# Softmax maxima negated on GpSimd between pieces of its other attention work; inverse of the denominators on VectorE

## What is computed

```python
scores = jnp.einsum('bthd,bshd->bhts', q, k)
mask = jnp.tril(jnp.ones((T, T), dtype=scores.dtype))
scores = scores * mask
attn = jax.nn.softmax(scores / T ** 0.5, axis=-1)
out = jnp.einsum('bhts,bshd->bthd', attn, v).reshape(B, T, H * Dh)
return out @ Wo
...
x = _layernorm(x + _L0_attn_ref(x, ...), axis=-1)
```

## Time and profile before

| | us |
|---|---|
| median of 3 runs | 1091.71 |
| lowest and highest | 1091.14, 1093.73 |
| span of the profiled execution (its own time isn't given apart from it) | 1090.9 |
| TensorE busy | 1037.0 |
| VectorE busy | 738.5 |
| ScalarE busy | 486.3 |
| GpSimd busy | 294.7 |

### The profile page before, as it was taken

How to read it: one execution, slowest core, us unless ns; L and a number is a source line. 1 busy time by engine, 2 the same in 40 slices (tenths; PEclk the granted TensorE clock), 3 DMA queues, 4 the chain that set the end, 5 groups by cost and what they waited for, 6 DMA issues and landing times.

```text
span 1090.9 us, 18063 instructions
## 1 busy us (share of the span) xinstructions
PE 1037.0 (95%) x6022; PEld 839.6 (77%) x6023; DVE 738.5 (68%) x1769; ACT 486.3 (45%) x905; POOL 294.7 (27%) x496
## 2 busy tenths in 40 slices
PE   7889998999999885999999999999999999999996
PEld 6667776777777664888888888888888888888885
DVE  5898699778868986566747546545565536654666
ACT  5688488758857884222324222131222122221124
POOL 2186348545733641223210006000000000000224
PEclk9999999999999998999999999999999999999998
DMA  8877267727743732224541003210020000100102
GB/s 260 237 200 204 78 199 200 197 83 188 199 117 117 207 143 77 79 77 164 175 162 61 1 1 40 39 39 1 1 77 12 27 0 33 45 1 1 39 27 89
DMA packets 55216, 106.18 MB, mean 97 GB/s; under 512 B 6240, under 2 KB 8288, under 8 KB 55136
## 3 DMA queue, kind: packets, MB, share of 16 engines
q1 hardware_dynamic: 50256, 90.99, 29.7%
q0 software_dynamic: 4880, 14.18, 3.4%
HBM read 72.11 MB, written 30.94 MB: 94 GB/s over the span
## 4 chain that ended last, share of the span: by engine, by line
PE 57%; DVE 2%; ACT 1%; issue 0%; DMA 0%; POOL 0%; POOLq 0%; DVEq 0%
PE f_bank L53 55%; PE f_bank L1714 1%; PE f_bank L1722 1%; PE f_bank L1793 1%; PE f_bank L1738 0%; DVE ln_stats L1104 0%; DVE rows_kept L2150 0%; ACT rows_kept L1132 0%; DVE h L2116 0%; DMA rows<-sorted_dram 0%; DVE rows_kept L2139 0%; DVE h L2056 0%; DVE rows_kept L1111 0%; POOL out L1660 0%; ACT fsg L1936 0%
## 5 line engine op out<-in xcount | busy, mean ns | idle before, releaser
L1896 ACT ACTIVATE fsg<-f_bank 128x512 f32<-128x512 f32 x64 | 38.2, 598 | 295.6 <-PE f_bank L53 289.2
L2056 DVE TENSOR_TENSOR h<-f_bank,fsg 128x512 f32<-128x512 f32 x64 | 44.2, 691 | 181.6 <-PE f_bank L53 181.4
L714 ACT ACTIVATE probs<-bank,nmax 128x384 f32<-128x384 f32 (+3 forms) x256 | 131.7, 549 | 21.4 <-DVE nmax L899 19.3
L883 DVE CUSTOM_DVE_ANT_0 bank<-bank,mask 128x384 f32<-128x384 f32 (+3 forms) x256 | 122.9, 502 | 13.8 <-PE bank L510 13.0
L521 PE MATMUL bank<-ident,probs 128*128 128x128 f32 x640 | 108.7, 284 | 24.6 <-DVE pt_lo L908 10.7
L1137 POOL TENSOR_SCALAR ln_var<-ln_mv 128x1 f32<-128x1 f32 x39 | 8.9, 229 | 438.8 <-DVE ln_mv L1106 437.4
L908 DVE TENSOR_TENSOR pt_lo<-bank,pt_hi 128x512 f16<-128x512 f32 (+1 forms) x192 | 114.7, 598 | 16.7 <-ACT pt_hi L724 16.4
L724 ACT ACTIVATE pt_hi<-bank 128x512 f16<-128x512 f32 (+1 forms) x192 | 104.9, 546 | 23.5 <-PE bank L521 22.9
L53 PE MATMUL bank<-x_hi,w_qk 128*128 128x512 f32 x256 | 101.5, 414 | 6.7 <-DVE x_lo L913 6.3
L53 PE MATMUL f_bank<-wd_hi,hs_lo 128*128 128x512 f32 x256 | 100.0, 391 | 0.0
L53 PE MATMUL f_bank<-wd_lo,hs_hi 128*128 128x512 f32 x256 | 99.9, 390 | 0.0
(11 more groups left out here) (275 smaller groups left out, 2445.7 us busy)
## 6 DMA issues: line engine op xcount, KB each, us to landing
big_lo<-q_hi_dram SPq DMA_DIRECT2D x32, 256.0 KB
big_lo<-q_lo_dram SPq DMA_DIRECT2D x32, 256.0 KB
big_lo<-k_hi_dram SPq DMA_DIRECT2D x32, 256.0 KB, 3.8
big_lo<-k_lo_dram SPq DMA_DIRECT2D x32, 256.0 KB, 5.1
rows<-sorted_dram SPq DMA_DIRECT2D x19, 256.0 KB, 2.6
q_hi_dram<-q_hi SPq DMA_DIRECT2D x16, 256.0 KB, 3.0
q_lo_dram<-q_lo SPq DMA_DIRECT2D x16, 256.0 KB, 2.9
k_hi_dram<-k_hi SPq DMA_DIRECT2D x16, 256.0 KB, 3.5
```

The source lines that it names most:

```text
L714: ins = act.activation(probs[u % RP][:, at:at + cols(r)], S[u % SR][:, at:at + cols(r)], ACT.Exp, bias=nmax[:, r, c:c + 1])
L883: dve.tensor_tensor_reduce(out=S[u % SR][:, at:at + cols(r)], in0=S[u % SR][:, at:at + cols(r)], in1=mask[:, T - cols(r):T], scale=1.0, sc ...
L1896: act.activation(fsg[v % 2][:, :], GB[v % 2][:, :], ACT.Silu).then_inc(s_sg, 1)
L2056: dve.tensor_tensor(h[r % 2][:, j, :], UB[v % 2][:, :], fsg[v % 2][:, :], ALU.mult).then_inc(s_h, 1)
```

## The change

The negated maxima of units 4 to 47 of each batch move from VectorE to GpSimd; units 0 to 3 stay on VectorE. `negated` now takes the engine. A case for units 24, 27 and 30, in which VectorE negated two columns in two instructions, falls away. GpSimd's attention work is written anew as a loop over units: the negation of u+2 first, and behind it whatever stands at that unit. The sums of head c come at unit 3c+6, the low parts of the next x at units 23, 25, 26 and 28, and `norm_heads` for group m is cut into four steps at units 16, 17, 19 and 20, each plus 12m. Its inverse is now a reciprocal on VectorE at units 17, 29 and 41 (`heads_inverse`), and the constant of -1 is gone. The statistics of row block 3 and the scatters of row blocks 2 and 3 move from behind a batch into units 3 and 6 of the next one. TensorE, ScalarE and SyncE have the same instructions in the same order.

```diff
+        x_lo_at = {23: 0, 25: 1, 26: 2, 28: 3}
+        SUMS_BEHIND = 2 * UPH
+        NORM_FROM = SUMS_BEHIND + (HPT - 1) * UPH + 1
...
+            def norm_step(b, m, step):
...
+                if step == 0:
+                    pool.wait_ge(s_c, b * NM + m + 1)
+                    pool.tensor_tensor(den[:, :, hs], c_up[:, :, hs], n_up[:, :, hs], ALU.mult).then_inc(s_t[0], 1)
...
+                elif step == 1:
...
+                    pool.tensor_tensor(o_tmp[0][:, :, :, :], tail, above, ALU.mult).then_inc(s_t[0], 1)
+                elif step == 3:
...
+                    pool.tensor_tensor(o_here, o_here, o_tmp[0][:, :, :, :], ALU.add).then_inc(s_t[0], 1)
+                elif step == 4:
...
+                    pool.tensor_tensor(o_raw[:, :, hs, :], o_raw[:, :, hs, :],
+                                       rinv[:, :, hs].unsqueeze(3).broadcast_to([P, NB, HPT, HD]),
+                                       ALU.mult).then_inc(s_on[0], 1)
...
             for b in range(B):
                 more = b < B - 1
...
+                for u in range(UPB):
+                    if AHEAD_S < u + AHEAD_MAX < UPB:
+                        negated(pool, b, u + AHEAD_MAX)
+                    if b > 0 and u == LAST_ROW_AT + 1:
+                        ln.rstd(pool, b * NB - 1, NB - 1)
+                    if b > 0 and u - 1 in rows_at:
+                        place(b - 1, rows_at[u - 1])
+                    if u in x_lo_at and more:
+                        x_lo(b + 1, x_lo_at[u])
+                    if u % UPH == 0 and u >= SUMS_BEHIND:
+                        head_sums(b, (u - SUMS_BEHIND) // UPH)
+                    if NORM_FROM <= u < NORM_FROM + (NM - 1) * UPM:
+                        norm_step(b, (u - NORM_FROM) // UPM, (u - NORM_FROM) % UPM)
...
+            def heads_inverse(b, m):
+
+                hs = slice(m * HPT, (m + 1) * HPT)
+                dve.wait_ge(s_t[0], (b * (NM - 1) + m) * 5 + 2)
+                dve.reciprocal(rinv[:, :, hs], den2[:, :, hs]).then_inc(s_t[0], 1)
...
-                    if fresh:
-                        negated(b, u + AHEAD_MAX)
+                    if fresh and u + AHEAD_MAX <= AHEAD_S:
+                        negated(dve, b, u + AHEAD_MAX)
+                    if u >= NORM_FROM and (u - NORM_FROM) % UPM == 1 and u < NORM_FROM + (NM - 1) * UPM:
+                        heads_inverse(b, (u - NORM_FROM) // UPM)
```

More of the change, by code:

```diff
@@ L265, in sum_parts, with negated, last_heads_normed @@
             eng.tensor_tensor(o_raw[:, :, c, :], part[0], part[1], ALU.add).then_inc(s_os[side], 1)
-        def norm_heads(eng, side, b, m):
-            per_batch = (NM - 1, 1)[side]
-            n = (b * per_batch + (m if side == 0 else 0)) * 5
+        def negated(eng, b, u):
+            m, h, rows = units[u]
+            c = m * HPT + h
+            rs = slice(rows[-1], rows[0] + 1, 2) if len(rows) > 1 else slice(rows[0], rows[0] + 1)
+            eng.wait_ge(s_mx, (b * HEADS + c) * NB + rows_done[u % UPH])
+            if rows[0] < NB - 1:
+                eng.tensor_scalar(nmax[:, rs, c:c + 1], smax[:, rs, c:c + 1], 0.0, -1.0, ALU.max,
+                                  ALU.mult).then_inc(s_nm, 1)
+            else:
+                eng.tensor_scalar(nmax[:, rs, c:c + 1], smax[:, rs, c:c + 1], -1.0, None,
+                                  ALU.mult).then_inc(s_nm, 1)
+        def last_heads_normed(eng, b):
+            m = NM - 1
+            side = 1
+            n = b * 5
             hs = slice(m * HPT, (m + 1) * HPT)
@@ L285, in norm_heads @@
             link(eng.tensor_tensor(den[:, :, hs], c_up[:, :, hs], n_up[:, :, hs], ALU.mult))
[L286 to L290, removed]
-            link(eng.tensor_tensor(den2[:, :, hs], den[:, :, hs], rsum[:, :, hs], ALU.add))
[L292 to L297, removed]
+            link(eng.tensor_tensor(o_tmp[side][:, :, :, :], tail, above, ALU.mult))
+            sum_parts(eng, side, b, HEADS - 1)
+            eng.wait_ge(s_os[1], PRIMED + 3 * (b + 1))
+            eng.wait_ge(s_os[0], PRIMED + 3 * (b + 1) * ALONE)
+            link(eng.tensor_tensor(den2[:, :, hs], den[:, :, hs], rsum[:, :, hs], ALU.add))
+            link(eng.reciprocal(rinv[:, :, hs], den2[:, :, hs]))
             link(eng.tensor_tensor(o_raw[:, 0:NB - 1, hs, :], o_raw[:, 0:NB - 1, hs, :], o_tmp[side][:, :, :, :],
@@ L366, in _ @@
                 more = b < B - 1
[L367 to L379, removed]
+                for u in range(UPB):
[11 more added lines that the diff above has]
+                        norm_step(b, (u - NORM_FROM) // UPM, (u - NORM_FROM) % UPM)
+                for c in range((UPB - SUMS_BEHIND) // UPH, ALONE):
+                    head_sums(b, c)
                 if more:
@@ L1041, in batch @@
                         lo(b + 1, 0)
-                        negated(b + 1, AHEAD_S)
+                        negated(dve, b + 1, AHEAD_S)
             def qk_lo(i):
```

66 lines of the change are left out of this document (31 added, 35 removed).

## The result

| | before | changed |
|---|---|---|
| median of 5 runs each, us | 1092.1 | 1098.11 |
| lowest and highest | 1091.14, 1093.73 | 1095.88, 1099.53 |
| ratio, 95% interval | | 1.0053 [1.0039, 1.0067] |
| profiled execution: span (its own time) | 1090.9 | 1094.2 (1095.88) |
| VectorE, GpSimd busy | 738.5, 294.7 | 730.4, 295.3 |

A forecast was written before the change was run, and what follows sets the result against it. TensorE was taken as nearly full beside projection pieces; from the last batch's unit 21, VectorE, ScalarE and TensorE handing banks round set the pace. 2.7 + 1.2 + 0.8 - 0.65 = +4.05 on 1091.7 gave 1095.8 us, range 1090.5 to 1099.5.

The forecast's parts named there:

- Boundaries: Three batch boundaries: unit 6's negation behind statistics and scatter on GpSimd makes its exponential 0.9 us late; 2.7 us lost.
- Each sign that it named: Each boundary: GpSimd's negation of unit 6 ends behind a scatter, ScalarE waits about 0.9 us, unit 6's transposes with it.
- First batch: Units 21 to 30: VectorE's second reciprocal waits 2.1 us for denominators on GpSimd's queue; 1.2 us lost, bounds 0.4 and 2.3.
- late negations of units 29 to 33: First batch: negations on the same GpSimd queue, counted with 0.8 to 1.0 us coming through to make 1.2 us.
- Unit 24: Second batch: the negation stands behind the first scatter of padding, and its exponential waits; 0.8 us lost.
- Relief in the last batch: Late half: one negation of every three is in TensorE's waiting ring; eight rings of 0.08 us, 0.65 us gained.
- 0.08 us slot: On VectorE a negation's 145 ns overlap the next instruction, which begins 0.08 us after it.
- The rival by which 3.5 us come back: Last batch's late half: each negation holds VectorE its full time, boundaries cost nothing; 1088.2 us, faster, chance 0.08.
- No relief in the full stretches: Where projection pieces stand between units, TensorE is nearly full and hides VectorE's relief, worth nothing.
- Each handover on the path: Rival: all 176 negations cost 229 instead of 145 ns on the path, 15 us; 1106 us, chance 0.04.
- The price of GpSimd's small operation: GpSimd's negation takes about 0.23 us; well over that on the two-column form would make the prediction wrong in size.
- The 0.8 us around the span: Span 1090.9 us against a run median of 1091.7: 0.8 us lie around the span and don't change.

The follow-up runs named there:

- e2: Changed kernel, but VectorE negates units 4 to 8 of the batches behind the first; 1093.53 us, ratio 1.0011 to before.
- e8: Changed kernel with the two late scatters of a batch issued six units later on GpSimd; 1093.96 us, ratio 1.002 to before.
- e5: Changed kernel with VectorE's reciprocal one unit later and the first pad at head 8 instead of 5; 1095.39 us, ratio 1.0037 to before.
- e10: Changed kernel with late scatters six units later, reciprocal one unit later, first pad at head 8, routing steps resumed two units later; 1093.79 us, ratio 1.0014 to before.
- e1: Changed kernel with all negations back on VectorE, GpSimd's new order and VectorE's reciprocals kept; 1096.79 us, ratio 1.0048 to before.
- e6: Kernel before, with negations of units 24, 27 and 30 as one 128x2 instruction instead of two one-column ones; 1095.4 us, ratio 1.0034.
- e4: e1 with negations of units 21, 24, 27, 30 of the first three batches as two one-column instructions; 1092.74 us, ratio 1.0005 to before.
- e9: Changed kernel; VectorE negates to unit 30 (first two batches) or 8 (others), one-column at 21, 24, 27, 30, reciprocal one unit later; 1091.07 us, ratio 0.9993.

## Why the prediction was right, and where not

It said 1095.8 us, in a range of 1090.5 to 1099.5, and slower with 0.51. The median is 1098.11, inside the range and slower. The mechanism that it named, GpSimd's queue ahead of a negation, is the one that the runs show; that the sum of its terms comes out as measured in attention is luck, as shown below.

- **Boundaries**, forecast 2.7 us, within 0.9 to 4.2: 2.81 at the edges, plus 0.57 at unit 4, which the prediction thought to have just enough room (ScalarE waits 0.78 to 0.80 us there at each boundary). Each sign that it named is there: the negation behind the scatter, ScalarE waiting 0.82, TensorE 1.09. e2 and e8 show both halves of the cause: the loss goes when VectorE negates, and also when GpSimd does but the scatter stands later.
- **First batch**, forecast 1.2, within 0.4 to 2.3: 1.48 to 1.55. The wait before the reciprocal was forecast at 2.1 us and was 1.75. With that wait gone (e5) half of the loss stays. Most of that half is the negation of unit 31 behind x_lo, 0.62 us in e5 and 0.59 in e10; the prediction had the "late negations of units 29 to 33" in its term, at 0.2 to 0.4 us. What it lacked is the held routing steps. The row of 408 ns that it quotes was a sign of them: that negation, at 183.79 in the trace of before, ends at 184.20, 0.03 us behind GpSimd's `o_raw`.
- **Unit 24**, forecast 0.8, within 0 to 1.2: 0.88 to 0.99; e5 removes it by moving the pad.
- **Relief in the last batch**, forecast 0.65 gained: 0.53, against 0.11 when VectorE negates everything (e1), so some 0.4 is the relief. The 0.08 us slot was the right row: TensorE's transposes that wait for a low part, three units apart, came 3.96 and 3.92 us apart in the late half before (from 388.77 on) and come 3.83 us apart now (from 392.44 on). The rival by which 3.5 us come back is out.
- **No relief in the full stretches**: 0.68 and 0.63 us were gained in the second and third batch. e6, which has nothing of the change, gains the same 0.66 behind its loss in the second batch, and e4, with all negations on VectorE, 0.50 and 0.52. So at least most of it is no relief by GpSimd's negations. A wait for a low part in the kernel before goes as soon as the engines stand otherwise to each other; what sets it I did not isolate.
- **"Each handover on the path"** is out: 176 negations at 234 ns, and ScalarE waits for one in only ten places.
- **The price of GpSimd's small operation** on the two-column form, which the prediction named as its risk, was 0.22 to 0.29 us, as taken.
- **The 0.8 us around the span** was a misreading: it set the span of one execution beside the median of others. Where the record gives both for one execution they differ by 1.7 us (1095.88 and 1094.2). The sum starts from the median, so nothing in it hangs on this.

The sum of the ledger, +4.01, is that of the prediction, +4.05, and that is luck. Its errors cancel: 0.7 us too little at the boundaries and 0.3 in the first batch, with 0.3 more from unit 24 and the last batch, against 1.3 us of gains not foreseen. The time moved by more, some 5.8 us by the ratio. What is missing is **open**: the changed kernel's two traces and the ten kernels made from it all lie above what their ledger adds to before, by 0.4 to 1.8 us (e9: -0.8 by its ratio, -1.66 by its ledger), while e6, made from before, lies 0.7 below. Part of the common sign may be the one trace of before, against which all are set: with the same 1.7 us its execution took some 1092.6 us, 0.5 above the median. What lies ahead of head 0 and behind the last head is 732.6 us in that trace and 733.0 on average in the twelve, but from 730.7 to 734.7 among them; head 0 alone comes 0.83 us before that of before in e8 and 1.37 behind it in e4. With one trace of each I can't place the rest.

## What to carry to other kernels

A cheap instruction that others wait for takes on the length of whatever can stand ahead of it on its new queue. List that queue's longest entries, above all DMA issues, and look at each place where the receiving engine has no lead. Before an instruction is moved to or beside GpSimd, look at the VectorE instructions that will run at the same time: a TENSOR_SCALAR in SBUF of 2 or of 19 columns was held to the end of a large GpSimd operation, and one column at a time was not. A special case in tuned code whose reason isn't written down is worth an experiment of its own before it is dropped or crossed.

## What the runs showed of the hardware that was not expected

- A VectorE TENSOR_SCALAR of 128x2 in SBUF, 0.15 us alone, took 0.43 to 1.70 us beside operations of GpSimd of 128x384 and 128x512 (e1); the same work as two of 128x1 took 0.20. One of 128x19 took up to 1.40 (e5) instead of 0.23.
- Short holds were in the kernel before already: seven of its two-column negations took 0.29 to 0.41 us, five of them beside an operation of 128x128.
- VectorE's maxima and low parts, which read PSUM, kept their 0.68 to 0.73 us for 512 columns beside such GpSimd operations, and the reciprocal of 128x16 its 0.24 to 0.25, though it too has one source and an even number of columns.
- The hold of 1.70 us outlasted one GpSimd operation: x_lo ended at 172.42 and the next began at 172.38, and VectorE's instruction ended at 172.87, 0.04 us behind that next one.
- In attention a scatter or pad keeps GpSimd for 0.96 to 1.27 us, with 0.15 to 0.82 us of issue ahead of it, and everything behind it in the queue waits for both.
